# Decoder block on one core: one program block for front and layers, an inverse norm in eight steps, and a new order of work within each tile's step

## The reference, cut to what matters

```python
x = x + causal_attention(layernorm(x))          # one head of 128
x = x + cross_attention(layernorm(x), ctx)      # 16 heads of 8, exp features
x = x + stack(layernorm(x))                     # six layers:
for i in range(6):
    s = shift_tokens(x)      # half of the channels comes from the token before
    q, k, v = split(s @ Wqkv[i])                # 16 heads of 64
    q, k = l2norm(q) * q_scale, l2norm(k) * k_scale      # then rotary
    x = local_attention(q, k, v) @ Wo[i] + x    # windows of 32, looks one back
    h = layernorm(shift_tokens(x)) * g + b
    a, gate = split(h @ W1[i] + b1)             # 341 wide each
    x = (a * gelu(gate)) @ W2[i] + b2 + x
```

## Time and profile before

| | |
|---|---|
| time, median of 3 runs | 1762.85 us (1761.89 to 1767.2) |
| the profiled execution | 1765.81 us, its span 1763.9 us |
| busy share of the span | PE 92%, PEld (weight loads) 75%, DVE 87%, ACT 74%, POOL 77% |
| granted TensorE clock, mean | 0.970 |
| chain that ended last | PE 67%, DVE 6%, issue 5%, DMA 4%, ACT 3% |
| inverse-norm steps per tile | 10 on DVE |

### The profile page before, as it was taken

One profiled execution on the slowest core, in us unless ns is written; L12 is line 12 of the kernel. 1 busy time (PEld: TensorE's weight loads), 2 busy tenths in 40 slices (PEclk: granted clock), 3 DMA queues, 4 the chain that ended last, 5 costly groups with the idle time before them and its releaser, 6 DMA issues.

```text
span 1763.9 us, 65318 instructions
## 1 busy us (share of the span) xinstructions
PE 1626.0 (92%) x26583; PEld 1331.2 (75%) x26583; DVE 1540.3 (87%) x3223; ACT 1305.8 (74%) x2473; POOL 1363.3 (77%) x972
## 2 busy tenths in 40 slices
PE   6688959999999999999999999999999999999996
PEld 4445537777788888787878888887888888888875
DVE  6578769998999999899999999998999998999981
ACT  4455647787887787787778778877877887787773
POOL 4355658788888888888888888888888888888863
PEclk9779979999999999999999999999999999999998
DMA  3734311110311211312213121213112122111111
GB/s 105 262 132 173 109 42 48 45 41 26 112 41 48 61 44 35 100 44 53 55 41 95 43 53 44 61 35 113 43 37 61 45 88 60 41 44 52 36 41 54
DMA packets 81085, 117.71 MB, mean 67 GB/s; under 512 B 41692, under 2 KB 55189, under 8 KB 80661
## 3 DMA queue, kind: packets, MB, share of 16 engines
q1 hardware_dynamic: 80210, 113.27, 21.9%
q10 hardware_dynamic: 578, 0.26, 0.1%
HBM read 38.72 MB, written 21.32 MB: 34 GB/s over the span
## 4 chain that ended last, share of the span: by engine, by line
PE 67%; DVE 6%; issue 5%; DMA 4%; ACT 3%; SPq 1%; POOL 1%; ACTq 0%; DVEq 0%; POOLq 0%
PE banks L1195 9%; PE banks L1182 9%; PE banks L1100 8%; PE banks L1144 7%; PE banks L1102 6%; PE banks L1101 6%; PE banks L1122 5%; PE banks L1240 4%; PE banks L1157 4%; DMA low<-w_low 4%; PE banks L1112 3%; PE banks L1212 2%; PE banks L1214 2%; PE banks L1213 2%; DVE qk_c L1524 1%
## 5 line engine op out<-in xcount | busy, mean ns | idle before, releaser
L1439 POOL TENSOR_TENSOR qk_c<-qk_c,qk_s 128x1024 f32<-128x1024 f32 x192 | 459.3, 2392 | 156.7 <-DVE qk_s L1535 156.6
L1447 POOL TENSOR_TENSOR qk_c<-qk_c,nrm 128x1024 f32<-128x1024 f32 x192 | 362.5, 1905 | 30.5 <-DVE nrm L1583 30.5
L1100 PE MATMUL banks<-high,xT 128*128 128x512 f32 x576 | 271.0, 471 | 29.4 <-DMA low<-w_low 14.1
L1524 DVE TENSOR_TENSOR qk_c<-banks,rot 128x512 f32<-128x512 f32 x384 | 262.2, 683 | 19.0 <-ACT sq L1307 17.7
L1535 DVE TENSOR_TENSOR qk_s<-banks,rot 128x512 f32<-128x512 f32 x384 | 261.8, 682 | 0.0
L1307 ACT ACTIVATE sq<-banks 128x512 f32<-128x512 f32 x384 | 240.3, 626 | 16.9 <-PE banks L1102 8.2
L1542 DVE TENSOR_REDUCE ssq<-sq 128x16 f32<-128x1024 f32 x192 | 232.4, 1211 | 0.0
L1102 PE MATMUL banks<-high,xT 128*128 128x512 f32 x576 | 229.8, 399 | 0.0
L1101 PE MATMUL banks<-low,xT 128*128 128x512 f32 x576 | 228.9, 397 | 0.1
L1349 ACT COPY pbd<-banks 64x512 f32<-64x512 f32 x192 | 111.8, 582 | 156.8 <-PE banks L1157 156.3
L1455 POOL TENSOR_TENSOR prob<-prob,pinv 128x512 f32<-128x512 f32 x192 | 196.4, 1044 | 13.5 <-DVE pinv L1619 4.3
(11 more groups left out here) (160 smaller groups left out, 3783.7 us busy)
## 6 DMA issues: line engine op xcount, KB each, us to landing
v_back<-v_own SPq DMA_DIRECT2D x96, 384.0 KB, 3.7
front_raw<-in_L_ffn_Wqkv_dram SPq DMA_DIRECT2D x18, 512.0 KB, 5.4
v_back<-v_own SPq DMA_DIRECT2D x72, 128.0 KB, 2.4
w_high<-high SPq DMA_DIRECT2D x15, 512.0 KB, 2.7
w_low<-low SPq DMA_DIRECT2D x15, 512.0 KB, 4.0
high<-w_high SPq DMA_DIRECT2D x15, 512.0 KB, 5.4
low<-w_low SPq DMA_DIRECT2D x15, 512.0 KB, 6.9
wo<-in_L_ffn_Wo_dram SPq DMA_DIRECT2D x6, 512.0 KB, 5.3
```

The lines of the kernel that those rows point to most:

```text
L1100: pe.matmul(bank[n % 2][:, :], xT[:, 1, lo:lo + P], w_hi[:, col:col + 512], start=True, stop=False)
L1439: pool.tensor_tensor(x, x, qk_s[:, kind, :], ALU.add).then_inc(s["rotd"], 1)
L1447: pool.tensor_tensor(x, x, bcast(nrm[:, t % 2, HEADS * kind:HEADS * (kind + 1)], 2, DH), ALU.mult).then_inc(s[("qn", "kn")[kind]], 1)
L1524: dve.tensor_tensor(qk_c[:, t % 2, kind, 512 * half:512 * half + 512].rearrange("p (h d) -> p h d", d=DH), bank[n % 2][:, :].rearrange("p ...
```

## The change

1. One block: `front` and `stack` return five programs each, and one block runs on each engine the first and then the second. In place of the barrier stand single waits: `copy_x` waits for a row of `front` (`rows_in`), PE for one memset and 15 of `front`'s 16 last sums, and POOL does the other five memsets (`zero_edges`) at t = 0, when `front` has read what they overwrite; SP's loads, `transpose_q(0)` and `store_values(0)` wait for those. Tiles that both programs hold (qk_c, xT, nrm and others) are allocated once; `front`'s two probability tiles are laid on qk_s.
2. The inverse norm: a scaled guess and two quadratic factors that depend on one product, eight steps in place of ten, with step 5 waiting for step 3 and step 6 for step 4.
3. The order in the bodies: on PE `transpose_k(., 0)` behind `project(t-1, 4)`, `transpose_x` behind `project(t, 2)`, `ffn_value(., 0)` behind `project(t, 0)`; on ACT `store_values(., 0)` first, `copy_x` near the end, `store_q` ahead of `squares(t, 2)`; on DVE `prob_sum` ahead of the second `square_sum`, and `prob_inv` and then the statistics behind it; on POOL `low_x` between the halves of `normalise_prob`, and one `ffn_product` behind them.

The diff without changes of indentation, cut to its core:

```diff
+            first = front(nc, part, ctx, a, k)
+            second = stack(nc, part, a, k, out)
+            with nc.Block() as block:
+                @block.vector
+                def _(dve):
+                    first[4](dve)
+                    second[4](dve)
...
 # PE's body
                 project(t - 1, 4)
+            transpose_k(t - 2, 0)
                 project(t - 1, 5)
...
-                transpose_x(t + 2)
                 project(t, 2)
+            transpose_x(t + 2)
...
-                transpose_k(t - 1, 0)
-            pe.wait_ge(s["zeroed"], 6)
+        pe.wait_ge(s["zeroed"], 1)
+        pe.wait_ge(k["s_front_added"], BATCH * GPB - 1)
 # ACT's body
+            exponentials(t - 3, 1)
...
-                store_att(t - 4, 0)
                 store_values(t - 1, 0)
+            store_att(t - 4, 0)
...
-                copy_x(t + 3)
...
-                squares(t, 2)
                 store_q(t - 1, 0)
                 store_q(t - 1, 1)
+            squares(t, 2)
                 squares(t, 3)
...
+            copy_x(t + 3)
...
-                exponentials(t - 2, 1)
 # POOL
+        def zero_edges():
+            pool.wait_ge(k["s_front_combined"], BATCH * GPB)
+            pool.wait_ge(k["s_rows_in"], BATCH)
+            pool.wait_ge(k["s_front_skip"], 16 * BATCH)
 # DVE: root steps
-                    dve.wait_ge(s["root"], done + n)
+                dve.wait_ge(s["root"], done + (n if n not in (5, 6) else n - 1))
...
+            elif n == 3:
+                ins = dve.tensor_tensor(c, u, y, ALU.mult)
+            elif n == 4:
+                ins = dve.scalar_tensor_tensor(out=u, in0=c, scalar=ROOT_QUAD[0][0], in1=c, op0=ALU.add, op1=ALU.mult)
+            elif n == 5:
+                ins = dve.scalar_tensor_tensor(out=w, in0=c, scalar=ROOT_QUAD[1][0], in1=c, op0=ALU.add, op1=ALU.mult)
```

More of the change, by code:

```diff
@@ L224, in front @@
     eq = sb("eq", [P, 2, 2, SEQ])
-    pa = sb("pa", [P, 2, SEQ])
-    paT = sb("paT", [P, 2, SEQ])
+    pa, paT = (k["qk_s"][:, n, :].rearrange("p (a s) -> p a s", a=2) for n in range(2))
     xd = sb("xd", [P, 2, 2 * CW])
@@ L391, in queries_and_values @@
                 if b == 0:
-                    pe.wait_ge(s_prepped, 1)
+                    prepare_features()
                 else:
-                    pe.wait_ge(s_pa, GPB * (b - 1) + 3)
-                pe.wait_ge(s_xnT, b + 1)
-                pe.matmul(bank[4][:, :], mqk[:, :], xnT[:, b % 2, :], start=True, stop=True).then_inc(s_qp_p, 1)
-                for j in range(GPB):
-                    last = pe.matmul(bank[5][:, P * j:P * j + P], xnT[:, b % 2, P * j:P * j + P], wvT[:, :],
-                                     start=True, stop=True)
@@ L400, in queries_and_values @@
-                last.then_inc(s_va_p, 1)
-            def scores_row(b):
-                pe.wait_ge(s_qp, b + 1)
-                for i in range(GPB):
-                    if i == 2:
-                        pe.wait_ge(s_va, b + 1)
-                    if i == 3 and b > 0:
-                        pe.wait_ge(s_pa, GPB * b)
-                    pe.matmul(bank[3 + i][:, 0:P * (i + 1)], qp[:, P * i:P * i + P], xnT[:, b % 2, 0:P * (i + 1)],
-                              start=True, stop=True).then_inc(s_sc, 1)
@@ L901, in stack @@
     f_h = sb("f_h", [P, 3, SEQ])
+    xT, xs_part, sq, qk_c, qk_s, ssq, nrm, root_c = (
+        k[n] for n in ("xT", "xs_part", "sq", "qk_c", "qk_s", "ssq", "nrm", "root_c"))
     st = sb("st", [P, GPB, 6])
@@ new lines, in body @@
+        def body(it, j, t):
+            if t == 0:
+                zero_edges()
+            normalise(t - 1, 0)
+            if j == 1:
+                normalise_ffn(it - 2)
+            normalise(t - 1, 1)
+            rotate(t, 0)
+            if j == 0:
+                ffn_product(it - 3, 1)
+            if j == 1:
+                low_ffn(it - 2)
+            if j == 3:
+                ffn_product(it - 2, 0)
+            rotate(t, 1)
+            normalise_prob(t - 2, 0)
+            low_x(t + 3)
+            normalise_prob(t - 2, 1)
+            if j == 0:
+                ffn_product(it - 3, 2)
```

2276 lines of the change are left out of this document (1139 added, 1137 removed).

## The result

The changed kernel takes 1756.01 us (median of 9 runs, 1748.19 to 1758.74) against 1761.89 (9 runs): ratio 0.9959, 95% interval 0.9945 to 0.9973. It is faster, by 6 to 7 us instead of the 45.7 forecast, and 1756.0 lies outside the range of 1702 to 1746.

What follows compares the result with a forecast made beforehand. PE was taken to set the pace in full rows with FFN, DVE before FFN work. Terms 10.0 + 4.8 + 7.9 + 0 + 22 + 0 + 1 = 45.7 us off 1765.8 gave 1720.1, less 3.0 for the median: 1717 us, range 1702 to 1746.

Steps and rivals of the forecast that it cites:

- body j=1: Three waits after add_ffn shrink or go, together 1.0 us in each of 22 rows: 22 us, bounds 11 and 29.
- body j=0: 0.36 us gained at project(t, 0), about 0.35 lost as DVE waits for exponentials: 0 us, bounds -6 and +6.
- The seam: Between front and the layers, DVE gets its first layer work earlier: 10.0 us gained, bounds 8.0 and 10.3.
- The shorter chain: Inverse norm: 0.60 us less per tile in 8 tiles where DVE sets the pace, 4.8 us; nothing where PE does.
- (a): Body j=1: a projection now covers the wait of transpose_x for bank 7 to be emptied, 0.45 us.
- (b): Body j=1: ACT no longer idles before copy_x, saving about 0.1 us at transpose_q and 0.2 at transpose_k.
- (c): Body j=1: the wait of project(t, 0) for the copy of v_own goes, 0.25 us.
- Body j=3: Copying v_own first removes the wait of project(t, 0), 0.36 us in each of 22 rows: 7.9 us.
- Moved at no cost: transpose_k between two projections, and other moved operations, cost 0 us; bounds for transpose_k -14 to +9 over 92 bodies.
- more issue gaps: Rival, chance 0.12: a denser PE meets some 11 more gaps of 1 us each, giving 1728 us.
- the tail: At the end of the kernel, two exposed chains get shorter: 1 us, bounds 0 and 3.
- the rows give nothing: Rival, chance 0.22: waits on sin_part replace those removed; only seam, lead-in and tail give 15.8 us: 1747.

Runs made afterwards that it cites:

- e2: The changed kernel with the old order in the bodies and the ten-step inverse norm, leaving the one block alone; 1753.26 us, ratio 0.9943 to the kernel before.
- e1: The changed kernel with product c written to a bank and to SBUF, nine steps, none reading SBUF twice; 1736.65 us, ratio 0.9844 to the kernel before.
- e4: The changed kernel, one block and new order, with the ten-step inverse norm of before; 1757.55 us, ratio 0.9962 to the kernel before.
- e6: e1 with transpose_x, copy_x and low_x put back at their old places; 1738.13 us, ratio 0.9863 to the kernel before.
- e8: e1 with ACT copying the first half of attT ahead of the first half of v_own again; 1750.66 us, ratio 0.9934 to the kernel before.
- e11: e1 with transpose_k(., 0) back at the end of PE's body; 1739.75 us, ratio 0.9855 to the kernel before.
- e7: e1 with DVE's old order of prob_sum, prob_inv, second square_sum and statistics put back; 1749.31 us, ratio 0.9931 to the kernel before.
- e3: The changed kernel with the old order on all engines, keeping one block and the eight-step chain; 1760.75 us, ratio 0.9984 to the kernel before.

## Why the prediction was wrong

The largest term, 22 us for body j=1, came out as a loss of 9, and it failed at one step: the eight-step chain was priced as if its new steps 4 and 5 cost 0.18 to 0.20 us like the others. They took up to 1.3 us, and in body j=1 this fell on the one wait that had no room. A second, smaller step failed beside it: `copy_x` ahead of the exponentials was priced in body j=0 alone.

**The seam: right.** 10.0 us forecast; 0.57% = 10 us by e2. In the traces DVE's distance shrank by 10.4, and the ramp to the first `attend` took 42.09 us in e2 (226.78 to 268.87) instead of 40.01 (239.81 to 279.82), so 8.3 are left there, inside the bounds of 8.0 and 10.3. The interval of the ratio, 6 to 14 us, is wider than these bounds.

**The shorter chain: the step that failed.** "That makes 0.60 us per tile" priced every step at the 0.18 to 0.20 us of the earlier trace rows. None of those rows has two inputs from SBUF; the new steps 4 and 5 have, and no row of the old chain showed such a step. I had listed where each operation writes but never compared where its inputs lie. Measured: 0.37 and 0.46 us in the mean, and the lead-in gained 0.20 us per tile (13.92 to 13.72) instead of 0.60. The double reads are not all of that. Two of the four tiles take 13.54 us, no more than without double reads (13.50 to 13.54 in e1); the fourth takes 13.83, where step 5 takes 0.50 us, and the first 13.97, but e1's first takes 14.07. The rest is a cost of the new order, which the prediction had at nothing here: with ten steps a tile takes 14.11 us in it (e4) against 13.92 in the old (e2). What the shorter chain gives was right: from e4 to e1, which has nine steps, it is 0.59 us, in these tiles and in j=0.

**Body j=1: the mechanism was half right, and its cover was missed.** Of 1.0 us, e1 shows 0.75 (17.20 to 16.45), and e6 puts 0.65 of it on parts (a) and (b), for which I had 0.75. Part (c) is not seen: with v_own second again (e8) the body is 16.33 us, no longer, and `ffn_out` waits for `add_attention` in both. I named as bounds the time "from `add_ffn` through `sin_part`", but the wait that came was ahead of `ffn_out`, on `add_attention`, with 0.05 us of room in the kernel before. The stretched step put 1.17 us there (17.62 against 16.45), more than all the gains of this body. So 22 us forecast, 0.75 x 22 = 16 available, and 0.42 x 22 = 9 lost.

**Body j=3: right size, wrong account.** v_own first does give something: in e6, where `copy_x` stands at its old place, j=3 is 0.22 and j=0 0.11 us shorter than before, 0.33 x 22 = 7 us, for the 7.9 forecast; undone in e8, it costs 0.22 and 0.13. But I priced `copy_x` ahead of the exponentials only for DVE in j=0, and not for ACT's own copies in every body: 0.18 us each in j=0, 2 and 3, 12 us in 22 rows. This took all of it and more.

**Body j=0: right.** Its net is 0.1 us (14.59 against 14.48), inside the bounds. `prob_sum` waits 1.15 us where I had 1.4, and the 0.60 us of the shorter chain covers most of it (e4 without it: 0.6 us longer).

**Moved at no cost: nearly.** `transpose_k` is worth nothing that the times show (e11; 0.2 us in j=2). `ffn_product(., 2)` behind the probabilities is free only because `prob_inv` moved too (e7), as the prediction said.

**Gaps.** The rival of more issue gaps did not come. Before, steps of 0.7 to 2.05 us from one small multiply to the next stand inside the scores and `ffn_out` in 9 of 21 bodies j=1, once in every eighth body; from the fifth on each comes 0.2 us later in its body than the one before (9.63 to 10.53 us after `attend`). In the changed kernel each body j=1 without a wait for weights takes 17.5 to 17.8 us: the wait for `add_attention` has room for them. What 20 rows take beyond 20 quiet ones fell from 28.6 us (1234.6 - 20 x 60.3) to 16.8 (1236.6 - 20 x 60.99), and so rows that are 0.7 us longer make the 20 rows only 2.0 us longer. Why the gaps are there, and why they are fewer and shorter in e1 (six, 0.6 to 1.2 us), stays open.

**The account.** From the start of the last operation of `front` to the first `attend`: 41.88 us against 51.45, -9.6. The lead-in's eight bodies: 113.1 against 115.2, -2.1. The row between these and the 20 rows: 61.5 against 63.0, -1.5. The 20 rows: +2.0. From the 93rd `attend` to the end: 72.3 against 71.4, +0.9, so the 1 us of the tail did not come either. `front` in this execution: +3.1. Together, before rounding, -7.1, for the 7.0 between the two spans; without the chance of `front` some 10 us, while the ratio over all runs says 7.2 (0.41% of 1762, 5 to 10). Of the rivals "the rows give nothing", 1747, comes nearest, but its reason, a wait on `sin_part` behind each one that goes, was not what happened. And the time would be worse still without something that the prediction did not foresee: the longer rows alone would have cost 14 us, and 12 of them came back in what the rows take beyond quiet ones.

## What to carry to other kernels

Before a new chain of small DVE operations is priced from the old one's rows, write down for each where both inputs lie; if both are in SBUF and POOL is busy beside it, its cost is not its own 0.19 us but what is left of POOL's instruction (here up to 2.4 us long), and it can be more where several follow each other (3.26 us in e3). When waits are taken out of a stretch, list everything that the next shared bank needs, with its margin in the trace: an instruction that already starts 0.05 us after its releaser is where the gain stops. An operation that runs in an engine's idle time is free only there; moved to the end of a body it delays that engine's whole next body, so a move that helps one body in four is made in that one alone.

## What was not expected of the hardware

- A 128x32 operation on DVE takes 0.19 us with one input from a bank, and 0.31 to 1.33 us (in e3 once 3.26) with both from SBUF when a POOL instruction has started before it; each of the stretched ones ends within 0.07 us of the end of a POOL instruction. One more instruction per tile that writes the value to a bank too made the kernel 1.2% faster.
- A start that follows another engine's end by 0.10 us can still be marked "issue" (`ffn_out` in e7), so such a mark is checked against the ends on the other engines.
